# A graph network in one kernel: second dense and first pre stage between the blocks of the second sums, run marks and loads elsewhere

## The chip, the cores and the metric

One core of one Trainium2 chip. The time is the device time of one execution, in microseconds (us), as the median over runs. Engines: TensorE (PE; PEld are its weight loads), VectorE (DVE), ScalarE (ACT), GpSimd (POOL) and SyncE (SP). Each is programmed by hand and they are ordered by semaphores alone.

## The reference

3125 nodes with 128 features, 100000 edges sorted by `dst`, 13 weight blocks. Two SAGE layers, then two PNA layers:

```
mean = segment_sum(x[src], dst) / max(deg, 1)
h    = relu(x @ Ws1 + mean @ Wn1 + b1)                      # sage0
y    = h @ Ws2 + mean(h) @ Wn2 + b2                         # sage1, mean(h) over the same edges
x    = layernorm(x + y)
for l in 0, 1:                                              # PNA, residual on its input
    xi, xj = x @ Wpre[:F], x @ Wpre[F:]                     # pre
    e = xi[dst] + xj[src] + b_pre
    agg = [mean(e), max(e), min(e), std(e)] per dst         # sums and extremes
    out = [x, agg, agg * amp, agg * att] @ Wpost ... @ Wlin # post
    x' = layernorm(out) (relu in layer 0) + input
result = layernorm(x + x')
```

## The kernel before

The nodes are 25 blocks (`NT`) of 125 rows (`NB`), taken in 5 groups (`NG`) of 5 tiles (`GT`). A segment sum is a product with counts: for every pair of blocks a 125 x 125 matrix of edge counts. A block's 25 matrices are an 800 KB tile A, stored in DRAM as `counts`. The rows are split into three bf16 parts (`take_apart`, tile XS), so a block of sums is 25 x 3 = 75 matmuls of 128 columns, `add_block` at L1139.

The order of the stages, with the times of the profile:

- 0 to 401 us: the edges are sampled and the counts are made block by block (`make_block`), and the first sums (those of sage0) run along with them. A block's counts and its `picks`, which select a row for each edge's source in the scans, are stored to DRAM.
- 401.75: the last block of the first sums (L1189 waits for all the block's counts). Beside it VectorE runs `mark_runs` (L1623 to 1650, 398.9 to 410.6): where a node's run of edges begins in the 128 slices of edges; part of it (`whole`) is of use only for inputs that take a branch not taken here (`general_sums`; `flagged` loads the flag).
- 412 to 447: sage0. For each group TensorE turns X and the means (`dense`, L1424), ScalarE copies each turned tile group out (L815), TensorE multiplies it by the weights (L1432), all through one bank pair `turn`. VectorE adds the bias, cuts at zero and splits (`hidden`, L2073 to 2079).
- 447 to 594: the second sums, `sums(1, F)`, a `Fori` over pairs of blocks on TensorE (L1199 to 1209) and ScalarE (L789 to 802), which scales a block's sums and loads the A of the block after the next. Beside it VectorE's `draw_rest` (L1942 to 2036) lists the edges beyond the picks, and POOL gathers 25 + 3 small pieces of these lists (L1106 to 1112). VectorE then waits for the end of the sums.
- 597 to 626: sage1, as sage0, with residual and layer norm on VectorE (`result`, `scaled`, L2086 to 2110; the roots are taken on ScalarE). 627 to 642: `dense_pre` (L1383 to 1409), the pre stage of PNA layer 0 (pre0), whose output Y is stored as the gather table; `rows_ready` counts its groups.
- 643 to 1300: the main scan of layer 0 (`main_scan`). POOL gathers rows of the table four at a time (L1078), VectorE scans them for maximum and minimum (L2170), TensorE selects and lifts rows by the picks (L1267, L1279) and adds the blocks of its sums. It has 91 slots (`NSLOT`); `SPLIT_SLOT` and others say what is done in which. SP loads the picks into a ring of three parts of 640 KB at the slots' start. The scan's last rows go to `rest_history`; a short chain (carries, `fix`) follows, then POOL gathers the rows in which the nodes end, 25 gathers (L1044), 5 to each of 5 semaphores `ext_in`.
- `post(0)` to 1396, pre1 to 1413, then X + H on VectorE (L2178) ahead of the main scan of layer 1 (to 2071), `post(1)` to the end.

## Time and profile before

| | us |
|---|---|
| median of 3 runs (2171.25 to 2175.35) | 2171.25 |
| span of the profiled execution | 2193.7 |
| PE busy | 1471.8 |
| DVE busy | 1424.0 |
| POOL busy | 804.2 |
| ACT busy | 502.9 |

The profiled execution took 22.45 us more than the median, so its times are compared with each other and the median is given beside them. Share of the chain that ended last: DVE 36%, PE 31%, POOL 1%. Times in the rows count from the span's start; "idle before <-releaser" is how long an engine had waited and what ended the wait, "issue" means that the profile shows no cause. A matmul with f32 operands appears twice in a count (x10 for 5 products).

### The profile page before, as it was taken

What the parts mean: (1) busy time and instruction counts of PE and PEld (TensorE: products, weight loads), DVE (VectorE), ACT (ScalarE), POOL (GpSimd) and SP (SyncE); (2) the same over time, 40 slices, a digit from 0 to 9 for tenths busy, and PEclk for the clock granted to TensorE, in tenths of its full rate; (3) what the DMA queues carried; (4) which work ended last, traced back from release to release, by engine and by line L of the source; (5) the groups of instructions that cost most, each with busy time, mean ns of one, the idle gap of its engine ahead of it and who ended that gap; (6) DMA issues with size and microseconds to landing.
All of it is one profiled execution on the core that took longest, in us unless ns stands there. A gap on an engine that the chain in (4) does not pass through costs nothing.

```text
span 2193.7 us, 30278 instructions
## 1 busy us (share of the span) xinstructions
PE 1471.8 (67%) x11250; PEld 1048.3 (48%) x11250; DVE 1424.0 (65%) x2879; ACT 502.9 (23%) x1074; POOL 804.2 (37%) x831
## 2 busy tenths in 40 slices
PE   0277777667854777678677755457777777877553
PEld 0166777657842444445444543324444445544432
DVE  7899999691066665557556645666655566665447
ACT  3367677300031011111111110310111111111101
POOL 4400000032015455455554523155454555546230
PEclk9889898878986898889898887868888888888777
DMA  5223333234433455455555531344554555555320
GB/s 116 89 120 138 146 138 138 83 112 148 135 106 98 156 177 169 145 176 194 181 172 168 177 112 54 98 150 160 176 171 151 192 173 178 196 165 158 109 89 24
DMA packets 126239, 309.36 MB, mean 141 GB/s; under 512 B 21744, under 2 KB 73408, under 8 KB 125742
## 3 DMA queue, kind: packets, MB, share of 16 engines
q1 hardware_dynamic: 75216, 145.00, 18.7%
q10 hardware_dynamic: 23470, 105.20, 13.7%
q0 software_dynamic: 27440, 57.77, 9.8%
q8 instruction: 56, 0.92, 0.2%
q14 instruction: 57, 0.47, 0.1%
HBM read 167.18 MB, written 140.75 MB: 140 GB/s over the span
## 4 chain that ended last, share of the span: by engine, by line
DVE 36%; PE 31%; another core or an unknown queue 16%; issue 8%; DMA 4%; ACT 2%; POOL 1%; ACTq 1%; DVEq 0%; SPq 0%; POOLq 0%
PE ps L1139 14%; PE ps L1267 6%; DVE accs L2141 5%; DVE scanned L2170 4%; DVE accs L2123 4%; DVE scanned L1682 3%; DVE scanned L1679 3%; DVE scanned L1688 3%; PE ps L1279 2%; DMA A<-counts 2%; PE ps L1164 2%; PE ps L1367 2%; PE ps L1432 1%; DVE S L1655 1%
## 5 line engine op out<-in xcount | busy, mean ns | idle before, releaser
L1078 POOL DMA_INDIRECT scanned<-table,rest_idx x688 | 674.0, 980 | 796.7 <-DMA rest_history<-scanned 327.9
L1139 PE MATMUL ps<-big,A 125*128 125x128 bf16 (+1 forms) x7500 | 772.5, 259 | 104.6 <-issue 81.8
L1139 PEld LDWEIGHTS ps<-big,A 125*128 125x128 bf16 x7500 | 623.6, 104 | 249.6 <-issue 139.8
L1267 PE MATMUL ps<-S,big 126*128 126x500 bf16 (+1 forms) x1050 | 282.1, 413 | 264.1 <-DVE accs L2141 184.2
L2141 DVE TENSOR_TENSOR accs<-accs,ps 128x1000 f32<-128x1000 f32 (+1 forms) x154 | 166.8, 1083 | 402.4 <-remote 313.5
L2170 DVE SCALAR_TENSOR_TENSOR scanned<-scanned,rest_neg 128x256 f32<-128x256 f32 x688 | 331.8, 482 | 32.5 <-issue 6.0
L1267 PEld LDWEIGHTS ps<-S,big 126*128 126x128 bf16 x1050 | 102.6, 107 | 387.8 <-DVE accs L2141 205.7
L1164 PE MATMUL ps<-scanned 128*128 128x150 bf16 x1050 | 116.2, 253 | 76.1 <-DVE scanned L1688 75.1
L2123 DVE TENSOR_TENSOR accs<-accs,ps 128x1000 f32<-128x1000 f32 (+1 forms) x154 | 166.0, 1078 | 1.8 <-DVE MS L1796 1.1
L1096 POOL IOTA Y<- 128x784 int32 x1 | 0.8, 786 | 362.8 <-DVEq L1944 362.8
L1164 PEld LDWEIGHTS ps<-scanned 128*128 128x128 bf16 x1050 | 87.6, 132 | 92.5 <-issue 73.2
L752 ACT COPY MS<-ps 128x128 f32<-128x128 f32 x50 | 13.3, 265 | 513.3 <-remote 281.0
L777 ACT ACTIVATE A<-ps,tiny 128x450 bf16<-128x450 f32 x175 | 109.7, 635 | 88.0 <-PE ps L1164 50.2
L1279 PE MATMUL ps<-S,lift 128*128 128x500 bf16 (+1 forms) x350 | 101.9, 370 | 34.8 <-DVE accs L2123 20.1
L1367 PE MATMUL ps<-weights,scanned 128*128 128x384 f32 x200 | 88.8, 574 | 53.2 <-DVE scanned L2223 43.7
L891 ACT ACTIVATE scanned<-scanned 128x512 f32<-128x512 f32 x172 | 104.7, 621 | 65.6 <-DMA scanned<-table,rest_idx 59.3
L1682 DVE TENSOR_TENSOR scanned<-scanned,H 128x900 bf16<-128x900 bf16 x175 | 108.7, 621 | 0.0
L1679 DVE TENSOR_TENSOR scanned<-scanned,H 128x750 bf16<-128x750 f16 x175 | 95.2, 544 | 10.6 <-PE ps L1164 10.3
L864 ACT ACTIVATE operands_t<-operands_t 128x128 f32<-128x128 f32 x50 | 15.5, 309 | 373.0 <-DVE operands_t L1789 200.9
L762 ACT ACTIVATE A<-A,tiny 128x640 bf16<-128x640 bf16 x125 | 99.6, 819 | 0.4 <-DVE S L1655 0.4
L1688 DVE TENSOR_TENSOR scanned<-scanned,H 128x768 bf16<-128x768 bf16 x175 | 96.5, 552 | 0.0
L1367 PEld LDWEIGHTS ps<-weights,scanned 128*128 128x128 f32 x200 | 38.9, 216 | 79.2 <-DVE scanned L2223 52.0
(384 smaller groups left out, 1409.8 us busy)
## 6 DMA issues: line engine op xcount, KB each, us to landing
rest_history<-scanned SPq DMA_DIRECT2D x172, 512.0 KB
A<-counts ACTq DMA_DIRECT2D x75, 800.0 KB
S<-picks SPq DMA_DIRECT2D x60, 640.0 KB
picks<-S ACTq DMA_DIRECT2D x25, 800.0 KB
counts<-A ACTq DMA_DIRECT2D x25, 800.0 KB
scanned<-table,rest_idx POOLq DMA_INDIRECT x688
table<-Y SPq DMA_DIRECT2D x10, 320.0 KB, 2.6
S<-picks SPq DMA_DIRECT2D x10, 160.0 KB
```

Source lines behind the costliest of these rows:

```text
L1078: nc.gpsimd.indirect_dma_start(out=lanes[:, r, s, 0:F], out_offset=None, in_=tables[1 + l], in_offset=bass.IndirectOffsetOnAxis(ap=rest_id ...
L1139: m = nc.tensor.matmul(acc[:, bank, 0:width], A[0:NB, slot, a, :], XS[0:NB, a, c, 0:width], start=a == 0 and c == 0, stop=a == NT - 1 and ...
L1164: m = nc.tensor.matmul(acc[:, h, at:at + CODES], hot_s[:, h, :, t], hot_c[:, h, t], start=t % WT == 0, stop=t % WT == WT - 1)
L1267: m = nc.tensor.matmul(ps[:, bank + h, 0:len(blocks) * NB], XS[0:NB + 1, a, c, 0:F], pick[0:NB + 1, part % RING, 0:len(blocks), a % PART, ...
L1279: m = nc.tensor.matmul(ps[:, bank + h, 0:len(blocks) * NB], lift[:], pick[:, part % RING, 0:len(blocks), a % PART, 0:NB], start=False, sto ...
L1367: m = nc.tensor.matmul(acc[:, b % GT, 0:3 * F], lhs_ext[:, SLOT[b % GT], h * P:(h + 1) * P], weights[:, w + 4 + 3 * h:w + 7 + 3 * h, :] .r ...
L1679: v.tensor_tensor(plain_s[:, h, 0:NB], iota_s[:, 0:NB], by_step(lows, n).unsqueeze(1).to_broadcast([P, NB, PT]), ALU.is_equal)\
L1682: v.tensor_tensor(hot_c[:, h].rearrange("p t (c u) -> p t c u", u=2), iota_c.rearrange("p (c u) -> p c u", u=2).unsqueeze(1) .to_broadcast ...
L1688: v.tensor_tensor(hot_s[:, h], plain_s[:, h], by_step(heavy, n).unsqueeze(1).to_broadcast([P, P, PT]), ALU.mult)\
L2123: v.tensor_tensor(top[:, :, 0:cols], top[:, :, 0:cols], ps[:, bank:bank + 2, 0:cols], ALU.max)\
L2141: v.tensor_tensor(low[:, :, 0:cols], low[:, :, 0:cols], ps[:, bank:bank + 2, 0:cols], ALU.min)\
L2170: v.scalar_tensor_tensor(this, last, rest_neg[:, i:i + 1], this, ALU.add, ALU.max)\
```

## The change

1. `mark_runs` moves from ahead of sage0 into `draw_rest`, and its `whole` part into the flagged branch. The last block of the first sums is split in five, each piece behind its counts (`add_block(0, NT - 1, ..., q * GT, (q + 1) * GT)`).
2. sage0 has two turn banks and four left-hand buffers, both products of a group run together (`turn_item`, `dense_product`), and blocks 0 and 1 of the second sums run piecewise between its groups (`first_pair`).
3. The second sums are written out block by block instead of a `Fori`. From block 16 (`DENSE_FROM`) sage1's turns and products, and pre0 in chunks of 4 tiles, run between the blocks; the last group, two chunks and five tiles of pre0 follow behind. ScalarE's `second_sums` and VectorE's `result`, `add_chunk`, `scaled` follow that order; the end of `draw_rest` becomes `place_rest`, behind them.
4. POOL waits for its 25 small gathers after every fourth.
5. SP loads the first picks as soon as they are stored, and those of layer 1 right behind main scan 0. ScalarE loads the first two A of each layer's sums at the end of the second sums and before `post(0)`.
6. The 25 gathers of `post` count on semaphores in runs of 1, 2, 4, 8, 10 (`END_RUNS`). The first split goes into slot 1 of the scan, X + H into its slot 0.

The diff, cut:

```diff
+XH_SLOT = 0
...
-SPLIT_SLOT = {1: 2, 3: 3, 5: 4}
+SPLIT_SLOT = {0: 1, 1: 2, 3: 3, 5: 4}
...
+DENSE_TURN = {"sage0": [4, 6], "sage1": [4]}
+CHUNK_TILES = 4
+CHUNKS = (NT - GT) // CHUNK_TILES
+DENSE_FROM = NT - 9
...
+END_RUNS = [range(0, 1), range(1, 3), range(3, 7), range(7, 15), range(15, NT)]
+END_RUN_OF = {b: i for i, r in enumerate(END_RUNS) for b in r}
...
+            def first_picks(l):
+                for n in range(RING):
+                    load_part(l, n)
             def main_scan(l):
                 loads = {}
-                for n in range(NPARTS):
-                    loads.setdefault(0 if n < RING else LAST_USE[n - RING] + 2, []).append(n)
+                for n in range(RING, NPARTS):
+                    loads.setdefault(LAST_USE[n - RING] + 2, []).append(n)
...
             general_sums(0)
+            general_sums(1)
+            for w in range(2):
+                sp.wait_ge(a_stored[w], 16 * (1 + 2 * ((NT + 1 - w) // 2)))
+            first_picks(0)
+            sp.wait_ge(runs_marked, 1)
+            sp.dma_start(saved_idx, idx).then_inc(saved, 16)
+            sp.dma_start(saved_neg, neg).then_inc(saved, 16)
...
+                if l == 0:
+                    first_picks(1)
...
+            act.wait_ge(dense_in, 1)
+            load_block(0, 0)
+            load_block(1, 1)
+            for i in range(2 * NG):
+                lhs_copy("sage0", i)
             general_sums(1)
...
+                if l == 0:
+                    load_block(0, 0)
+                    load_block(1, 1)
...
+                if b % BATCH == BATCH - 1:
+                    pool.wait_ge(rest_in, 16 * (b + 1))
...
+            for q in range(NG):
+                pe.wait_ge(counts_made, (NT - 1) * NG + q + 1)
+                add_block(0, NT - 1, 2, 0, F, q * GT, (q + 1) * GT)
...
+                    if l == 0 and s == 0:
+                        pe.wait_ge(rows_ready, NG)
...
+                    run = END_RUNS[END_RUN_OF[b]]
+                    if b == run[0]:
+                        pe.wait_ge(main.ext_in[END_RUN_OF[b]], 16 * len(run) * (l + 1))
...
+            def turn_item(d, source, i):
+                g, banks = i // 2, DENSE_TURN[d]
+                if i >= len(banks):
+                    pe.wait_ge(copied, ITEM_BASE[d] + i - len(banks) + 1)
+                turn_tiles(dense_turn[banks[i % len(banks)]], source, g * GT, (g + 1) * GT).then_inc(turned, 1)
+            def dense_product(d, g, at):
+                pe.wait_ge(copied, ITEM_BASE[d] + 2 * g + 2)
+                pe.wait_ge(evac, EVAC_BASE[d] + g)
+                for t in range(GT):
+                    for q in range(2):
+                        m = nc.tensor.matmul(dense_out[:, t, :], lhs[2 * (g % 2) + q][:, t * P:(t + 1) * P],
+                                             weights[:, at + q, :], start=q == 0, stop=q == 1)
+                        if t == GT - 1:
+                            m.then_inc(product, 1)
+            def first_pair(g):
+                for b in range(2):
+                    if g == 0:
+                        pe.wait_ge(a_in[b], 16)
+                    pe.wait_ge(parts_ready, 2 + g)
+                    add_block(1, b, b, b, F, g * GT, (g + 1) * GT)
...
+            pe.wait_ge(dense_in, 1)
+            pe.wait_ge(sums_out, NT + 2)
+            turn_item("sage0", flat(X[:]), 0)
+            turn_item("sage0", flat(MEAN), 1)
+            for g in range(NG):
+                if g + 1 < NG:
+                    turn_item("sage0", flat(X[:]), 2 * g + 2)
+                    turn_item("sage0", flat(MEAN), 2 * g + 3)
+                dense_product("sage0", g, W_SAGE[0])
+                if g > 0:
+                    first_pair(g - 1)
+            general_sums(1)
+            first_pair(NG - 1)
+            for b in range(2, NT):
+                pe.wait_ge(a_in[b % 2], 16 * (1 + b // 2))
+                add_block(1, b, b % 2, b % 2, F, 0, NT)
+                j, odd = divmod(b - DENSE_FROM, 2)
+                if j < 0:
+                    continue
+                if not odd:
+                    if j > 0:
+                        dense_product("sage1", j - 1, W_SAGE[1])
+                    if j > 1:
+                        turn_chunk(j - 2)
+                    turn_item("sage1", flat(H[:]), 2 * j)
+                else:
+                    if j > 1:
+                        use_chunk(j - 2)
+                    pe.wait_ge(sums_out, NT + 2 + GT * (j + 1))
+                    turn_item("sage1", flat(MEAN), 2 * j + 1)
+            pe.wait_ge(sums_out, 2 * NT + 2)
+            turn_item("sage1", flat(MEAN), 2 * NG - 1)
+            use_chunk(CHUNKS - 3)
...
+            dense_product("sage1", NG - 1, W_SAGE[1])
+            for c in range(CHUNKS - 2, CHUNKS):
+                turn_chunk(c)
+                use_chunk(c)
+            pe.wait_ge(x1_ready, NG)
+            turn_tiles(dense_turn[0], flat(X[:]), NT - GT, NT).then_inc(pre_turned, 1)
+            pe.wait_ge(pre_copied, CHUNKS + 1)
+            pe.wait_ge(rows_ready, CHUNKS - 1)
...
                 dve.sem_inc(found, 1)
+                mark_runs()
+                dve.sem_inc(runs_marked, 1)
...
+                link(v.tensor_scalar(CHUNK, restI, P * REST - 1.0, 1.0, ALU.min, ALU.add))
                 dve.sem_inc(pe_go, 1)
-                dve.wait_ge(small_mm, 5)
-                link(v.tensor_scalar(lanem[:], turn_u[:, P:2 * P], BIG, -BIG, ALU.mult, ALU.add))
+            def place_rest():
+                dve.wait_ge(small_mm, 4)
+                link(v.tensor_scalar(lanem[:], rest_lanes, BIG, -BIG, ALU.mult, ALU.add))
...
             evacuate("sage0", hidden)
-            dve.sem_inc(parts_ready, 1)
+            general_sums(1)
             draw_rest()
...
             for g in range(NG):
-                result(g, mark, need, first=g == 0)
-            scaled(NG - 1, mark, need)
+                result(g, mark, need)
+                if g >= 2:
+                    add_chunk((0, 1, 3)[g - 2])
+                scaled(g, mark, need)
+                if g == NG - 2:
+                    add_chunk(2)
+            add_chunk(CHUNKS - 1)
+            split_rows(0, 0)
+            place_rest()
+            dve.wait_ge(pre_product, CHUNKS + 1)
+            link(v.tensor_tensor(tiles(Y[:], NG - 1), last_out, over_n(V_BPRE[0], GT), ALU.add))
+            dve.sem_inc(rows_ready, 1)
...
+                    if l == 1 and s == XH_SLOT:
+                        link(v.tensor_tensor(X[:], X[:], H[:], ALU.add))
+                        dve.sem_inc(xh_ready, 1)
```

Two places in the order of instructions. First, **TensorE, sage0** (`ident` turns a tile group, `weights` multiplies it, `big,A` is a block of the second sums). Before, the end of sage0 and the loop of the second sums:

```order
L1424 MATMUL ps<-ident,MS 128x128 x5
L1432 MATMUL ps<-weights,scanned 128x128 x5
L1207 UNCONDITIONAL_BRANCH
L1207 ISA
L1136 REGISTER_ALU
L1139 MATMUL ps<-big,A 128x128 x75
L1136 REGISTER_ALU
L1139 MATMUL ps<-big,A 128x128 x75
L1207 REGISTER_ALU
L1207 COMPARE_AND_BRANCH
```

Of the change, two groups of sage0:

```order
L1461 MATMUL ps<-ident,X 128x128 x5
L1461 MATMUL ps<-ident,MS 128x128 x5
L1478 MATMUL ps<-weights,scanned 128x128 x10
L1194 MATMUL ps<-big,A 128x128 x30
L1461 MATMUL ps<-ident,X 128x128 x5
L1461 MATMUL ps<-ident,MS 128x128 x5
L1478 MATMUL ps<-weights,scanned 128x128 x10
L1194 MATMUL ps<-big,A 128x128 x30
```

Each group now turns the next group's two items ahead of its own product, and 30 of the 150 matmuls of blocks 0 and 1 stand behind each product.

Second, **TensorE, end of the second sums.** Before, the last block, the three small matmuls and the first turn of sage1:

```order
L1139 MATMUL ps<-big,A 128x128 x75
L1444 MATMUL ps<-small,scanned 128x25
L1445 MATMUL ps<-small,scanned 128x24
L1446 MATMUL ps<-ident,tiny 128x128
L525 TENSOR_LOAD flagI
```

Of the change, blocks 21 and 22 with what runs around them (C holds the turned tiles of pre0):

```order
L1478 MATMUL ps<-weights,scanned 128x128 x10
L1461 MATMUL ps<-ident,X 128x128 x4
L1461 MATMUL ps<-ident,H 128x128 x5
L1194 MATMUL ps<-big,A 128x128 x75
L1505 MATMUL ps<-weights,C 128x128 x4
L1461 MATMUL ps<-ident,MS 128x128 x5
L1194 MATMUL ps<-big,A 128x128 x75
L1478 MATMUL ps<-weights,scanned 128x128 x10
```

Turns, products and chunks of pre0 stand ahead of blocks that wait for nothing but their A; before, all of them stood behind the last block.

## Rows read from the trace of the kernel before

**Rows 1.** Busy time by stretches; columns us, PE, PEld, DVE, ACT, POOL busy (instructions), PEclk, DMA share, GB/s

```profile
467.80:521.00 53.20, 36.24 (x451) 29.98 (x452) 33.56 (x56) 2.38 (x7) 31.14 (x28) 0.74 0.33 108
521.00:594.00 73.00, 69.44 (x1204) 67.41 (x1204) 0.00 (x0) 5.69 (x16) 0.00 (x0) 1.00 0.51 169
594.00:643.40 49.40, 31.95 (x229) 28.73 (x228) 29.98 (x108) 13.93 (x26) 0.00 (x0) 0.90 0.07 20
643.40:1300.20 656.80, 474.58 (x2820) 301.41 (x2820) 404.54 (x696) 101.92 (x256) 336.34 (x344) 0.86 0.51 166
```

**Rows 2.** Chain of waits, 385 to 455 us; columns start, us, what ran

```profile
401.75 7.10 PE ps L1139 x75
...
413.73 1.96 PE ps L1432 x10
...
417.54 2.50 PE ps L1432 x10
...
440.86 1.40 PE ps L1432 x10
...
447.37 4.76 DMA A<-counts
```

**Rows 3.** Timeline of ScalarE, 396 to 425 us; start, us, ..., [idle before <-releaser]

```profile
401.72 0.35 ACTq L768 DMA_DIRECT2D counts<-A  x1
...
412.99 0.69 ACT L815 COPY scanned<-ps 128x640 f32<-128x640 f32 x1 [3.73 <-PE ps L1424]
```

**Rows 4.** Timeline of TensorE, 385 to 486 us

```profile
439.37 0.71 PE L1424 MATMUL ps<-ident,MS 128*128 128x128 f32 x5
...
463.09 4.36 PE L1139 MATMUL ps<-big,A 125*128 125x128 bf16 x75 [0.85 <-DMA A<-counts]
...
485.41 0.58 PE L1139 MATMUL ps<-big,A 125*128 125x128 bf16 x4 [0.92 <-issue]
```

**Rows 5.** Timeline of POOL, 460 to 520 us

```profile
468.97 0.97 POOL L1107 DMA_INDIRECT icol<-rest_rows,icol  x1 [19.20 <-DMA rest_rows<-Y]
...
507.40 0.94 POOL L1112 DMA_INDIRECT Y<-rest_lists,slices  x1 [0.30 <-issue]
```

**Rows 6.** DMA queues, 467.8 to 521 us; packets, MB, share of 16 engines

```profile
q10 hardware_dynamic: 864, 4.92, 26.7%
q0 software_dynamic: 992, 0.54, 4.9%
```

**Rows 7.** DMA queues, 643.4 to 1300.2 us

```profile
q8 instruction: 22, 0.36, 0.2%
```

**Rows 8.** Chain of waits, 592 to 660 us

```profile
620.93 0.84 DVE Y L2092
...
626.40 0.83 DVE Y L2092
```

**Rows 9.** Timeline of POOL, 640 to 650 and 1412 to 1421 us

```profile
647.11 1.03 POOL L1078 DMA_INDIRECT scanned<-table,rest_idx  x1 [138.77 <-DMA table<-Y]
...
1413.12 1.09 POOL L1078 DMA_INDIRECT scanned<-table,rest_idx  x1 [70.34 <-DMA table<-Y]
...
1417.20 3.33 POOL L1078 DMA_INDIRECT scanned<-table,rest_idx  x1 [0.30 <-issue]
```

**Rows 10.** Chain of waits, whole span

```profile
1300.16 2.59 DMA rest_history<-scanned
...
1420.18 11.75 DMA S<-picks
...
2070.90 2.63 DMA rest_history<-scanned
```

**Rows 11.** Timeline of POOL, 1310 to 1318 us

```profile
1311.80 0.97 POOL L1044 DMA_INDIRECT big<-rest_history,icol  x1 [1.88 <-DMA rest_history<-fix,fixI]
...
1316.83 0.95 POOL L1044 DMA_INDIRECT big<-rest_history,icol  x1 [0.30 <-issue]
```

**Rows 12.** Waits: engine, tile and line, what released them; total us, times, longest us

```profile
DVE accs L2141 <- remote: 313.5, 46, 14.0
```

More of the change, by code:

```diff
@@ L468, in __init__ @@
                 self.fix_out = sem(name + "fix_out")
[L469 removed]
+                self.ext_in = [sem(name + "ext_in")] if looped else [sem(name + f"ext_in{i}") for i in range(len(END_RUNS))]
                 self.start = sem(name + "start")
@@ new lines, in use_chunk @@
+            def use_chunk(c):
+                pe.wait_ge(pre_copied, c + 1)
+                if c == 1:
+                    pe.wait_ge(x1_ready, 3)
+                elif c > 1:
+                    pe.wait_ge(rows_ready, c - 1)
+                for t in range(CHUNK_TILES):
+                    m = nc.tensor.matmul(chunk_out[:, t, :], x_turned[:, c * CHUNK_TILES + t, :],
+                                         weights[:, W_PRE[0] + 1, :], start=True, stop=True)
+                m.then_inc(pre_product, 1)
@@ L1446, in _ @@
-            nc.tensor.matmul(turn_u[:, P:2 * P], lane_whole.to_broadcast([P, P]), ident[:], start=True, stop=True)\
-                .then_inc(small_mm, 1)
-            general_sums(1)
-            dense(1, "sage1", [flat(H[:]), flat(MEAN)], [W_SAGE[1], W_SAGE[1] + 1],
-                  [(0, F, True, False), (0, F, False, True)])
-            for l, inp in ((0, X), (1, H)):
-                dense_pre(l, f"pre{l}", flat(inp[:]), (x1_ready, h_ready)[l])
+            pe.wait_ge(dense_in, 1)
+            pe.wait_ge(sums_out, NT + 2)
@@ new lines, in _ @@
+            dense_product("sage1", NG - 1, W_SAGE[1])
[6 more added lines that the diff above has]
+            pe.wait_ge(rows_ready, CHUNKS - 1)
+            for t in range(GT):
+                m = nc.tensor.matmul(last_out[:, t, :], x_turned[:, NT - GT + t, :], weights[:, W_PRE[0] + 1, :],
+                                     start=True, stop=True)
@@ L1453, in _ @@
+            m.then_inc(pre_product, 1)
+            for l in range(2):
+                if l == 1:
+                    dense_pre(1, "pre1", flat(H[:]), h_ready)
                 main_scan(l)
@@ L1894, in general_sums @@
                     if g > 1:
-                        for i in range(NG):
-                            dve.wait_ge(main.ext_in[i], 16 * GT * (g - 1))
+                        for i, run in enumerate(END_RUNS):
+                            dve.wait_ge(main.ext_in[i], 16 * len(run) * (g - 1))
                         dve.sem_inc(reload_ask, 1)
```

298 lines of the change are left out of this document (147 added, 151 removed).

## The prediction

> **What bounds the kernel now.** I first read the busy times by stretches, to see which stages could give time at all, then the chain of waits, to see what ends each of them, and last the timelines of the engines at the places that the change touches.
>
> The stretches [rows 1] tell three things. From 521 to 594 us, in the second sums, TensorE is busy 69.44 of 73.00 us at a granted clock of 1.00: 1204 matmuls, so 60.6 ns each and 4.55 us for a block's 75. That part is bound by TensorE. From 467.8 to 521 us the same loop does 451 matmuls in 53.20 us. At 60.6 ns they need 27.3, so 25.9 us are lost, at a clock of 0.74. From 594 to 643.4 us no engine is full: TensorE 31.95, VectorE 29.98 and ScalarE 13.93 of 49.40 us, and the DMA share is 0.07. There the engines wait for one another in turn, which is what another order of work can mend. The scan from 643.4 to 1300.2 us has POOL, VectorE and TensorE interleaved; the change leaves its body alone.
>
> What are the 25.9 us? TensorE stands idle or creeps ("<-issue", [rows 4]: 4 matmuls in 0.58 us, where 75 took 4.36 at 463.09), while POOL issues 28 gathers between 468.97 and 508.3 [rows 5]. The block loads moved 4.92 MB in that time and POOL's queue only 0.54 MB [rows 6], so it isn't bandwidth. The stall goes with POOL issuing indirect transfers whose landing nobody awaits.
>
> In the chain [rows 2], the last block of the first sums (75 matmuls, 7.10 us) starts only when all its counts are made; the dense stage follows, then a bare load of 4.76 us, then the second sums. The main scans run from POOL's first gather to the last store: 647.11 to 1300.16 and 1413.12 to 2070.90 [rows 9, 10].
>
> **The sum** is made against the profiled execution, whose span is 2193.7 us. That is 22.45 above the median of 2171.25, and I take that offset over unchanged.
>
> *Stage A, until block 2 of the second sums starts (463.09 before, [rows 4]).* The last block in five pieces: the store of its counts is issued at 401.72 [rows 3], so the last piece is cast by then, and 15 matmuls (7.10 x 15/75 = 1.4) end at 403.1 instead of 408.85. `mark_runs` leaves the path here (it goes into `draw_rest`, beside the second sums). ScalarE then waits for that store (about 4.8, as the load of the same 800 KB, 4.76 [rows 2]), issues two loads and reaches its first copy at about 409 instead of 412.99 [rows 3]. Both turns are ready, so two copies (0.69 each) and both slow products (1.96 + 2.50, the first group's before [rows 2]) end at 414.9 instead of 420.0. From there a group costs TensorE two turns of 0.71 [rows 4], two products of 1.38 to 1.40 [rows 2] and now 30 matmuls of blocks 0 and 1 at 58 ns (4.36/75), together 5.93 us. Before, the last product ended at 442.26, four groups after the first, 5.55 each. VectorE's 5.0 us a group (442.26 to the load's issue at 447.3) fit under 5.93. So the last product ends at 414.9 + 23.7 = 438.6, its group is split at 443.6, and block 2's load follows the last pieces of block 0: 1.1 + 4.8, start at 449.6. **Gain 13.4.** The wait for the first loads of A disappears, since they were issued before the first copy.
>
> *Stage B, blocks 2 to 24.* Before: 463.09 to 593.8 = 130.7 us, of which 23 x 4.55 = 104.6 are work and 26.1 the stall. After: POOL waits for its landings after every fourth gather. No row shows that wait's effect. Bounds: it changes nothing (26 lost), or it removes all of it (0). I take 5 lost, because the same loop loses nothing as soon as POOL is silent [rows 1], and at most four gathers are in flight now. Added on TensorE before the last block: 9 turns (9 x 0.71 = 6.4), 4 products (4 x 2.76 = 11.0), 3 chunk turns of 4 tiles (1.7) and 2 chunk products (2.0): 21.1. They absorb about 1.8 of waits for A. Sum 104.6 + 5 + 21.1 - 1.8 = 128.9. **Gain 1.8**, and the last block ends at 578.5. So the interleaving alone costs here; what it buys comes next. The gathers move with `mark_runs` (11.7 us, 398.9 to 410.6, now ahead of them on VectorE) and have six waits of a landing each; VectorE should be ready at about 533, as TensorE gives the first of sage1's products. From then a group is due every two blocks (9.1 us), and VectorE needs 5.47 (626.40 - 620.93, [rows 8]) and short adds, so it catches up 3 us a group.
>
> *Stage C, from the last block to the last row of the first table.* Before 49.4 us [rows 1]. After: the last MEAN turn, copy, chunk, small matmuls and product 6.5; VectorE's group 5.5 and root 0.5, so the last `x1_ready` 12.5 after the last block. Then VectorE adds chunk 4, splits and places (0.7 + 2.6 + 1.5 = 4.8), which covers TensorE's last turn, copy and product (2.8), and the last add is 0.85: 18.2. **Gain 31.2**, the largest term. Rows are ready at 596.7 instead of 643.2.
>
> *Main scans and post stages.* Picks loaded early don't start layer 0's scan sooner, since its first rows come by POOL's gathers: 0, with bounds -2.6 (the split that moved into slot 0) and +5. The 25 gathers for `post` come 1.26 us apart (1311.80 to 1316.83 for four, [rows 11]), and the first group was due after five. With runs of 1, 2, 4, 8, 10 it is due after one: 4 x 1.26 = 5.0, of which I count 4, for each layer. In layer 0 the early picks of layer 1 (three of 640 KB) and two A loads (800 KB) now collide with that chain of short transfers. The nearest row is the gather at 1417.20, which took 3.33 instead of about 1 us beside such loads [rows 9]; I take 3 off. **Post 0: +1** (bounds -8 to +5), **post 1: +4**.
>
> The Trainium skill ("DMA: Bandwidth & Descriptors", section "Queues, rings and completion order") says that a DMA engine goes round its queues a packet at a time, so a short transfer would wait for a packet, not for a load. By that the toll is under 1 instead of 3, and the saving 2 larger. The row at 1417.20 speaks against it, so I keep 3.
>
> Layer 1's scan waited 11.75 us for picks at 1420.18 [rows 10], and it had 3.5 us of X + H before it. Yet it took only 657.8 us from POOL's first gather to its end, against 653.1 in layer 0: the scan absorbs most of that. **+3**, with bounds 0 and 15.
>
> Sum: 13.4 + 1.8 + 31.2 + 1 + 3 + 4 = 54.4. Profiled 2139.3, median **2117**. That is far over the 0.2% (4.3 us) that a measurement of this kernel can tell from no change.
>
> **The rivals.**
> 1. *The stall beside the gathers stays, or is only in profiled executions.* For: no row shows that the wait on `rest_in` helps, and the offset of 22.45 between profile and median is close to 21. Against: VectorE's waits of the same kind inside the scans total 313.5 us [rows 12], far above 22.45, so such stalls are no artifact of profiling. Either way 21 us of the gain go: 2138. Chance 0.20.
> 2. *Slower: straight-line code stalls TensorE on instruction fetch.* The loop over 23 blocks becomes 23 x 75 x 2 = 3450 instructions. TensorE's fetch queue brought 22 packets for 5640 instructions (2820 matmuls with their weight loads) in the first scan [rows 1, 7], so 256 a packet, and 13.5 packets are added, one per 9.7 us of sums. Its price if all the scan's unexplained waits were fetches: 313.5 over the two scans' 44 packets = 7.1 us each. Then 13.5 x 7.1 = 96 is lost and 54 gained: 2213. It decides above 54/13.5 = 4.0 us a packet. Against: the stretch from 467.8 to 521 stalls in a loop that fetches nothing new. Chance 0.06. The Trainium skill ("Runtime: NRT & Kernel Launch", section "Instruction fetch mechanics") has blocks of 256 instructions too and calls the cost of crossing one mostly hidden; by that this rival's price is about 0.
> 3. *VectorE comes late.* A landing beside two queued block loads can take 9.5 (2 x 4.76) instead of 2.5 us; six of them add 42 to POOL, so VectorE starts sage1's groups at 575, and stage C keeps about four groups of 5.47: 22 less, minus what A's waits give back, 2131 to 2140. Against: the gathers' data is 0.54 MB. Chance 0.09.
> 4. *The order changes but another wait takes it all up*: 2171. Nothing in [rows 1] speaks for it; 0.01.
>
> **How the numbers follow.** The forecast has 0.64. Its own range is 2098 (18.6 more: scan 1 by 12, post 0 by 4, no split cost 2.6) to 2131 (post 0 by 9 and scan 1 by 3 worse, 2 more in C). The range to 2146 takes in rivals 1 and 3, the first with 8 us of such costs besides, and leaves out rival 2 and the tails. Faster 0.64 + 0.20 + 0.09 = 0.93, same 0.01, slower 0.06.
>
> **What would show it.** Right: TensorE without gaps while POOL gathers at about 475 to 525; last block of the second sums ending near 579; POOL's first scan gather near 600 instead of 647.11; no wait for S<-picks at the start of layer 1's scan; `post`'s first turn of EXT one landing behind the first of the 25 gathers, not behind the fifth. Wrong: matmuls in fours with "<-issue" gaps (rival 1 if beside gathers, rival 2 if they come with q8's packets all through the sums), VectorE's first add of sage1 after 570 (rival 3), or a scan whose length from first gather to last store grows over 653.1 and eats the earlier start.

## The result, and the profile after

| | before | changed |
|---|---|---|
| median, us | 2173.3 (4 runs, 2171.25 to 2180.13) | 2110.75 (4 runs, 2081.93 to 2119.21) |
| ratio | | 0.9623, 95% interval 0.9553 to 0.9692 |
| profiled span | 2193.7 | 2117.5 |
| TensorE's fetch packets (q8) | 56 | 69 |

Faster, by 62.5 us between the medians and by 82 by the ratio, which leaves the two runs of the changed kernel with the lowest clock out. The interval of the ratio is 67 to 97 us; 54 were forecast. By the ratio the time is 2091 us, below the range's low end of 2098.

Busy time by stretches, changed kernel (columns as in [rows 1]): blocks 2 to 16 of the second sums, blocks 17 to 24 with the work between them, and the stage behind them.

```profile
446.40:527.60 81.20, 69.19 (x1127) 66.45 (x1128) 52.08 (x91) 5.14 (x14) 29.52 (x28) 0.96 0.53 174
527.60:579.80 52.20, 49.56 (x727) 49.06 (x726) 15.40 (x59) 10.08 (x21) 0.00 (x0) 0.97 0.38 127
579.80:606.30 26.50, 19.62 (x111) 17.06 (x111) 17.23 (x53) 12.47 (x21) 0.00 (x0) 0.76 0.27 82
```

The stage behind the sums fell from 49.4 [rows 1] to 26.5 us. Timeline of TensorE, changed kernel, at the places of stage A and the tail (beside [rows 4]):

```profile
400.47 4.36 PE L1194 MATMUL ps<-big,A 125*128 125x128 bf16 x75 [1.84 <-ACT A L792]
...
411.86 2.69 PE L1478 MATMUL ps<-weights,scanned 128*128 128x128 f32 x20
...
446.47 10.18 PE L1194 MATMUL ps<-big,A 125*128 125x128 bf16 x150 [3.14 <-DMA A<-counts]
...
579.61 2.45 PE L1478 MATMUL ps<-weights,scanned 128*128 128x128 f32 x20
...
586.73 2.05 PE L1505 MATMUL ps<-weights,C 128*128 128x128 f32 x8 [2.07 <-DVEq L2233]
...
589.85 4.08 PE L1478 MATMUL ps<-weights,scanned 128*128 128x128 f32 x20
```

Block 2 starts at 446.47 (forecast 449.6). The rows at 579.61 and 589.85 are the products of sage1's groups 3 and 4: group 3's comes only behind the last block. The row at 586.73 is a chunk of pre0 that waits for VectorE to add the chunk before it. Timeline of POOL, changed kernel (beside [rows 9, 11]): the first gather of either scan, the two transfers of the fix and the first of the 25 gathers.

```profile
609.11 0.94 POOL L1130 DMA_INDIRECT scanned<-table,rest_idx  x1 [92.24 <-DMA table<-Y]
...
1254.93 1.03 POOL L1085 DMA_INDIRECT fix<-rest_history,fixI  x1 [30.20 <-DMA rest_history<-scanned]
1263.16 1.03 POOL L1090 DMA_INDIRECT rest_history<-fix,fixI  x1 [7.21 <-DVEq L1969]
1265.85 0.97 POOL L1096 DMA_INDIRECT big<-rest_history,icol  x1 [1.66 <-DMA rest_history<-fix,fixI]
...
1366.56 1.12 POOL L1130 DMA_INDIRECT scanned<-table,rest_idx  x1 [69.74 <-DMA table<-Y]
```

And the start of layer 1's scan, before and after (timeline of VectorE). I count the first slot from its `take_low`, in which VectorE takes over the slot's minimum (the rows at 1441.51 and 1374.61). It lay 28.4 us behind POOL's first gather (1413.12, [rows 9]) and lies 8.0 behind it now, with X + H following instead of leading.

```profile
1416.23 3.49 DVE L2178 TENSOR_TENSOR X<-X,H 128x3200 f32<-128x3200 f32 x1
1434.84 1.20 DVE L2120 COPY accs<-ps 128x1000 f32<-128x1000 f32 x1 [15.12 <-PE ps L1267]
1441.51 1.20 DVE L2138 COPY accs<-ps 128x1000 f32<-128x1000 f32 x1 [4.57 <-remote]
```

```profile
1374.61 1.19 DVE L2275 COPY accs<-ps 128x1000 f32<-128x1000 f32 x1
1375.72 3.48 DVE L2337 TENSOR_TENSOR X<-X,H 128x3200 f32<-128x3200 f32 x1
```

### The profile page after: what moved, and what is told of

It reads as the page before. It is cut to its first block, busy times and chain, and to the rows that moved or that the text cites. A ratio compares the mean times of both kernels' runs of the same rounds, so it can differ in the third digit from the quotient of the medians.

```text
span 2117.5 us, 30101 instructions
## 1 busy us (share of the span) xinstructions
PE 1474.9 (70%) x11248; PEld 1055.0 (50%) x11248; DVE 1422.7 (67%) x2870; ACT 502.6 (24%) x1075; POOL 807.6 (38%) x831
## 3 DMA queue, kind: packets, MB, share of 16 engines
q1 hardware_dynamic: 75216, 145.00, 19.4%
q10 hardware_dynamic: 23470, 105.20, 14.2%
## 4 chain that ended last, share of the span: by engine, by line
PE 33%; DVE 33%; another core or an unknown queue 16%; issue 11%; DMA 3%; POOL 2%; ACT 2%; ACTq 1%; DVEq 0%; POOLq 0%
PE ps L1194 15%; PE ps L1307 6%; DVE accs L2278 5%; DVE scanned L2307 4%; DVE accs L2260 3%; DVE scanned L1796 3%; DVE scanned L1793 3%; DVE scanned L1802 3%; PE ps L1319 2%; PE ps L1220 2%; PE ps L1410 1%; PE ps L1278 1%; PE ps L1280 1%; DVE S L1769 1%
## 5 line engine op out<-in xcount | busy, mean ns | idle before, releaser
L1410 PE MATMUL ps<-weights,scanned 128*128 128x384 f32 x200 | 91.7, 589 | 54.4 <-DVE scanned L2361 40.9
L782 ACT COPY MS<-ps 128x128 f32<-128x128 f32 x50 | 13.3, 265 | 457.9 <-PE ps L1194 256.4
L1793 DVE TENSOR_TENSOR scanned<-scanned,H 128x750 bf16<-128x750 f16 x175 | 95.1, 544 | 12.3 <-PE ps L1220 12.2
```

Source lines behind the costliest of these rows:

```text
L1410: m = nc.tensor.matmul(acc[:, b % GT, 0:3 * F], lhs_ext[:, SLOT[b % GT], h * P:(h + 1) * P], weights[:, w + 4 + 3 * h:w + 7 + 3 * h, :] .r ...
L1793: v.tensor_tensor(plain_s[:, h, 0:NB], iota_s[:, 0:NB], by_step(lows, n).unsqueeze(1).to_broadcast([P, NB, PT]), ALU.is_equal)\
```

## The experiments

The runs fell on chips of two kinds, and this decides how each is read. On three chips the kernel before took 1782 to 1784 us, and its traces show no wait on a releaser that they can't name. In the other three sets of runs (the result's, r5 to r8, r17 and r18) it took 2139 to 2173, and in either kernel VectorE waited some 240 to 310 us in the scans on a releaser that the trace doesn't show (line of the waits' view, changed kernel, beside [rows 12]):

```profile
DVE accs L2278 <- remote: 240.0, 41, 12.8
```

I call them chips without and with the stall. Medians are only compared within a chip. "Scan body" is from the first slot's `take_low` to the end of the last slot.

### The two kernels again

> The kernel before, for a trace from the same chip as the runs beside it. If the scans' bodies (first slot to last) differ by chip and not by kernel, they take here what the changed kernel's take on this chip, within 10 us; the first slot of layer 1's scan comes 28 us after POOL's first gather on any chip.

> The changed kernel on the same chip. Stage by stage against the kernel before: block 2 of the second sums 17 us earlier, rows ready 37 to 50, the start of layer 1's scan 20 shorter, the bodies of the scans equal within 10 us each. If instead the change shortened the bodies, both are 7 us or more shorter here too.

> The changed kernel once more, to see how far its runs spread. If the extra gain over the forecast (the two main scans together 41 us shorter than before, where 3 were forecast) belongs to the change, the scans are again about 642 and 628 us from POOL's first gather to the last store. If a part is chance of the run, the bodies behind the first slots (about 634 and 620 us) come back nearer to 641 and 629, and the time lies 10 to 20 us higher. The ratio to before should be 0.960 to 0.976.

r9 and r10 ran on one chip without the stall: 1782.24 and 1755.29 us, ratio 0.9845 (0.9817 to 0.9872). r1, on another such chip: 1751.66, 0.9833 (0.9805 to 0.9860), where 0.960 to 0.976 was expected from the result; its scans can't be held against the result's. Stretches of r9, then of r10, each with blocks 2 to 14, blocks 15 to 24, the time behind the sums and the start of layer 1's scan:

```profile
457.90:518.30 60.40, 56.09 (x975) 54.46 (x975) 37.78 (x73) 4.72 (x13) 30.48 (x28) 1.00 0.60 196
518.30:563.20 44.90, 43.10 (x750) 41.88 (x751) 0.00 (x0) 3.36 (x10) 0.00 (x0) 1.00 0.49 165
563.20:619.00 55.80, 34.49 (x235) 30.81 (x232) 33.48 (x112) 17.90 (x31) 0.05 (x1) 0.84 0.13 35
...
1184.10:1209.40 25.30, 6.17 (x18) 2.56 (x18) 8.41 (x9) 6.55 (x11) 19.77 (x19) 0.53 0.74 252
```

```profile
440.80:506.00 65.20, 59.08 (x976) 57.71 (x976) 44.50 (x67) 4.78 (x13) 24.69 (x24) 0.95 0.55 184
506.00:567.70 61.70, 57.93 (x875) 57.42 (x875) 23.00 (x82) 10.46 (x22) 4.46 (x5) 0.97 0.44 143
567.70:596.90 29.20, 22.33 (x128) 18.39 (x125) 18.71 (x55) 14.60 (x24) 0.00 (x0) 0.77 0.28 86
...
1169.90:1177.90 8.00, 5.25 (x18) 2.30 (x18) 2.37 (x4) 5.40 (x9) 6.17 (x7) 0.79 0.16 43
```

The kernel before loses almost nothing beside its 28 gathers here: 975 matmuls in 60.40 us at a clock of 1.00, where the recorded chip lost 25.9 us. So the change costs TensorE 21.6 us from block 2 to block 24 (457.9 to 563.2 against 440.8 to 567.7) and gives 26.4 back behind it (up to POOL's first gather). POOL's first gather came 22 us earlier (619.0 against 596.9); 37 to 50 were expected, and the difference is the 21.6. The scan bodies are 6.7 and 4.8 us longer in the changed kernel (459.6 and 461.1 against 466.3 and 465.9): a split moved into both, X + H into the second. r1's were 462.1 and 468.5. Layer 1's first slot came 25.2 us behind its gather in r9 (28 were expected) and 8.1 in r10.

### POOL's wait on its gathers

```diff
-                if b % BATCH == BATCH - 1:
-                    pool.wait_ge(rest_in, 16 * (b + 1))
```

> The changed kernel without POOL's wait after every fourth of the 25 small gathers. Theory (gathers in flight that nobody awaits stall the second sums): blocks 2 to 16 lose about 26 us again instead of 12.9, so rows are ready 10 to 13 us later. Rival (the wait does nothing, the loss depends on how the loads of A lie against the gathers): 606 within 3 us.

> The changed kernel without that wait, again. On a chip with the stall: theory 90 to 94 us for blocks 2 to 16, where five traces with the wait gave 76 to 85; rival 76 to 85. On a chip without: 75.

> The kernel before with nothing but POOL's wait after every fourth small gather. Theory on a chip that shows the stall (scan bodies over 600 us): blocks 2 to 16 take 13 us less than in the kernel before on this chip, about 81 instead of 94. Rival 1 of the forecast: no change, within 3 us. On a chip without the stall (bodies near 465 us) both say 0.

> The kernel before for a trace beside the next runs. On a chip with the stall (scan bodies over 600 us): blocks 2 to 16 of the second sums take about 94 us as in the recorded profile; on a chip without it about 69.

> The kernel before with POOL's wait after every fourth small gather, again. On a chip with the stall: theory 81 us for blocks 2 to 16 instead of 94; rival 1 of the forecast 94 within 3. On a chip without: 70 and 69, no difference in time.

All five fell on chips without the stall, where both theories say nothing happens, and nothing clear of noise did: r3 1747.44 us (0.9803, 0.9776 to 0.9829), r15 1753.9 (0.9846, 0.9817 to 0.9876), the kernel before with the wait added 0.9996 twice (r12, r14; 0.9979 to 1.0014 and 0.9975 to 1.0017), r13 as before 1783.84. Without the wait the changed kernel was 4.2 us faster on r1's chip (r3; the intervals overlap), so the wait costs little or nothing there. The last two runs, both on a chip with the stall, test it (r17 has three edits, told below; up to block 13 only the wait and the marks' place differ from r18):

> The changed kernel with sage1 from block 14, no wait of POOL on its small gathers, and the marks of the runs ahead of sage0. Theory: VectorE is free near 500 instead of 528 us, the stall of 8.3 us ahead of the second product (dense from 14 alone) goes, the stage behind the last block takes 20 instead of 29 us: rows ready about 8 to 10 us earlier than in the changed kernel, and so the whole time. Rival: something else in that stage takes it up (0 to 2 us). On a chip with the stall, blocks 2 to 14 lose 13 us more without the wait if the wait is what helped; if not, they take what the changed kernel's take within 4 us.

> The changed kernel on the same chip, to set the run before it against. Gather window and tail as in the runs so far: last matmul of the sums to POOL's first gather 29.4 us, first gather 7.9 us ahead of the first slot.

Timeline of TensorE and stretch of blocks 2 to 13 in r17 (no wait), then in r18 (wait):

```profile
466.51 2.07 PE L1194 MATMUL ps<-big,A 125*128 125x128 bf16 x34 [0.82 <-DMA A<-counts]
468.75 0.39 PE L1194 MATMUL ps<-big,A 125*128 125x128 bf16 x4 [0.17 <-issue]
...
489.86 0.73 PE L1194 MATMUL ps<-big,A 125*128 125x128 bf16 x10 [0.92 <-DMA A<-counts]
491.27 0.40 PE L1194 MATMUL ps<-big,A 125*128 125x128 bf16 x4 [0.68 <-issue]
```

```profile
445.70:525.00 79.30, 63.74 (x899) 58.43 (x900) 45.35 (x83) 4.04 (x11) 31.15 (x28) 0.83 0.41 134
```

```profile
473.47 0.49 PE L1194 MATMUL ps<-big,A 125*128 125x128 bf16 x6 [0.28 <-issue]
474.20 1.90 PE L1194 MATMUL ps<-big,A 125*128 125x128 bf16 x31 [0.24 <-issue]
476.79 8.55 PE L1194 MATMUL ps<-big,A 125*128 125x128 bf16 x150 [0.68 <-DMA A<-counts]
```

```profile
446.60:505.90 59.30, 53.64 (x900) 51.78 (x900) 44.47 (x67) 4.04 (x11) 22.09 (x20) 0.97 0.59 190
```

The same 900 matmuls take 79.3 us without the wait and 59.3 with it. Without it they often come in fours, as in [rows 4], while POOL gathers back to back (459.7 to 499), though not all the time: 152 of them run through from 476.74 to 488.9. With it the stall ends when POOL stands (timeline of POOL, r18), and doesn't come back beside the next eight gathers (477 to 492):

```profile
472.71 0.94 POOL L1160 DMA_INDIRECT icol<-rest_rows,icol  x1 [0.30 <-issue]
477.16 1.70 POOL L1160 DMA_INDIRECT icol<-rest_rows,icol  x1 [3.50 <-DMA icol<-rest_rows,icol]
```

Five more traces with the wait on such chips (the result's, r5 to r8) take 65.8 to 73.7 us for blocks 2 to 14; r18 takes 65.9, r17 84.3 and the kernel before 85.5. So with the wait this stretch is 11 to 20 us shorter, and the pair r17 and r18 lies at the upper end. r8 has the marks where r17 has them, but keeps the wait, and takes 73.7: the marks' place isn't what costs r17 its time.

### The work between the blocks

```diff
                 add_block(1, b, b % 2, b % 2, F, 0, NT)
+            for b in range(DENSE_FROM, NT):
                 j, odd = divmod(b - DENSE_FROM, 2)
-                if j < 0:
-                    continue
```

and the same on ScalarE.

> The changed kernel with sage1 and the chunks of pre0 in the same order and with the same banks, but all behind the last block of the second sums. Forecast's theory (the work between the blocks costs 19.5 us there and saves 31 behind them): rows are ready 12 us later, ratio to the changed kernel 1.005. Rival (VectorE's 5.5 us a group is the bound of that stage either way, and what saved time is that pre0 follows in chunks): the sums end about 21 us earlier (near 559), the stage behind them takes about 41 instead of 26.5 us, and rows are ready within 5 us of 606.

1764.2 us, ratio 0.9898 (0.9873 to 0.9923), against 1751.66 for r1 on the same chip. Stretches of r2 (block 2 to 24; behind the sums), then of r1:

```profile
443.70:552.90 109.20, 100.23 (x1726) 98.00 (x1727) 52.05 (x91) 8.09 (x22) 29.56 (x28) 0.98 0.57 191
552.90:615.00 62.10, 43.50 (x252) 37.59 (x249) 34.06 (x113) 21.67 (x37) 0.02 (x1) 0.78 0.14 41
```

```profile
445.70:570.20 124.50, 114.59 (x1849) 112.76 (x1850) 68.05 (x149) 15.23 (x35) 29.98 (x28) 0.98 0.50 168
570.20:599.80 29.60, 22.73 (x129) 18.79 (x126) 18.70 (x55) 14.61 (x24) 0.01 (x1) 0.77 0.28 85
```

With the work between the blocks (r1) the sums take 15.3 us more and the stage behind them 32.5 less. r2 is late by 15.2 at POOL's first gather, by 12.5 in the median. The account expected 12, and it holds. The rival, by which the chunks and banks alone save the time, expected about 41 us behind the last block and falls: it took 62.1.

### Sage1 two blocks earlier

`DENSE_FROM` is 14, so the product of group 3 and one more chunk stand ahead of the last block.

> The changed kernel with sage1 started two blocks earlier, from block 14, so that the product of group 3 and a chunk stand ahead of the last block. Theory (the stage behind the last block waits for VectorE's group 3, which starts only then): rows ready 6 to 10 us earlier, ratio to before 0.978 to 0.981 on a chip without the stall, where the changed kernel had 0.984. Rival (VectorE isn't free before 528 us, so the first product only waits and TensorE stalls between blocks): 0 to 2 us.

1757.6 us, 0.9842 (0.9820 to 0.9864), where 0.978 to 0.981 was expected: no gain over the changed kernel. The stage behind the sums is 20.0 us instead of 29.4, as expected, but ahead of the second product TensorE waits 8.3 us. The row names ScalarE's copy, and that copy stands behind a root that VectorE asks for in group 0, which it begins only at 535.62, when it is free of `draw_rest` (timelines of TensorE, VectorE and ScalarE, r16):

```profile
540.13 3.86 PE L1480 MATMUL ps<-weights,scanned 128*128 128x128 f32 x20 [8.32 <-ACT scanned L830]
...
535.62 0.82 DVE L2217 TENSOR_TENSOR Y<-ps,vectors 128x640 f32<-128x640 f32 x1
...
539.29 0.21 ACT L823 ACTIVATE small<-small 128x5 f32<-128x5 f32 x1 [11.73 <-DVEq L2185]
```

r17 adds the two edits that free VectorE early (marks ahead of sage0, no wait of POOL). That stall goes and the 20.0 us stay, but on its chip blocks 2 to 13 take 20 more, as told above: first gather at 614.0 instead of r18's 605.5, median 2106.79 against 2078.24 (ratios 0.9879, 0.9832 to 0.9926, and 0.9744, 0.9678 to 0.9809). Of these 28.5 us the traces account for the 8.5 up to the first gather; where the others lie isn't shown, for behind it r17's profiled execution is the shorter one. Sage1 from block 14 with the marks ahead and the wait kept wasn't tried.

### Where the marks are made

```diff
+            mark_runs()
             link(v.tensor_copy(ends_up_to, turn_u[:, P:2 * P]))
...
                 dve.sem_inc(found, 1)
-                mark_runs()
```

> The changed kernel with the marks of the runs ahead of sage0 on VectorE again (without their flagged part). Theory: VectorE isn't waited for before sage0's first sum at about 414.5, the marks end near 408, so sage0 starts as early as before; the small gathers start 6 us earlier. Rows ready within 2 us of 606; what left the path was the flagged part and the unsplit last block, not the marks. Rival (the forecast's wording: the marks leave the path): 6 to 8 us slower.

On a chip with the stall: 2084.16 us, 0.9729 (0.9673 to 0.9785). The marks end well before VectorE is wanted (timeline of VectorE, r8). Block 2 starts 47.2 us behind the start of the first sums' last block (397.50 to 444.70), against 46.0 in the changed kernel (400.47 to 446.47), so their place is worth about 1 us and not the rival's 6 to 8:

```profile
403.34 0.29 DVE L1884 COPY run_ends<-ps 128x128 f32<-128x128 f32 x1
411.74 0.82 DVE L2200 TENSOR_TENSOR H<-ps,vectors 128x640 f32<-128x640 f32 x1 [8.10 <-PE ps L1478]
```

### The start of layer 1's scan

> The changed kernel with the first picks of layer 1 loaded only behind the table's stores. Theory (the scan pays in full for what its first slot waits, because everything behind it follows in a fixed order): from POOL's first gather of layer 1 to the first slot 20 to 25 us instead of 8.0, and the time 12 to 17 us longer, less 3 for the collision ahead of post(0), so 9 to 14 longer. Forecast's theory (the scan absorbs most of it): the first slot is late, but the last store comes at most 4 us later.

> The changed kernel with X + H ahead of the main scan of layer 1 again, picks early. Theory of full price: 3.5 us longer. Rival: it lay beside the gathers and costs nothing, because the first slot waits for picks or rows; 0 within 1 us.

> The changed kernel with the first two A of each layer's sums loaded in the scans again instead of at the end of the second sums and ahead of post(0). Theory: they are needed from slot 6 on, so the scans don't change; the fix gather at the end of scan 0 still collides with the picks (it took 6.6 us, 3.7 before the change). 0 within 2 us. Rival: the bodies of the scans gained (about 7 and 9 us) because these 3.2 MB no longer fall on their first slots; then the scans are 5 to 15 us longer together.

These ran on one chip with the stall: 2082.19 us (0.9745, 0.9692 to 0.9798), 2100.99 (0.9818, 0.9764 to 0.9871) and 2089.61 (0.9703, 0.9627 to 0.9778). No changed kernel ran beside them, and their intervals are wider than what they test. But the stage itself reads clean: from POOL's first gather to the first slot 8.7, 12.2 and 10.6 us. No edit alone brings the old 28.4 back; for r5 alone 20 to 25 were expected. The scan bodies of r7 (612 and 613 us) are not longer than those of the other changed kernels, so its rival, by which the A loads' place gave the shorter bodies, isn't borne out. So I put two together: X + H ahead, then its store, then the picks.

> The changed kernel with the start of layer 1's scan in the old order: X + H first, its store, then the first picks. Theory (either part alone cost 0 to 4 us, since the other left room; together they are the old 28.4 us): first slot 20 us later than in the changed kernel, and the whole time 15 to 20 us longer, since the body doesn't absorb it. Rival (the forecast: the body absorbs most): first slot late, time 3 us longer.

1759.46 us, 0.9866 (0.9841 to 0.9891), on r10's chip (1755.29). The first slot comes 19.4 us behind the first gather instead of 8.1, held by the picks behind the store (chain of waits, r11; `before` has 11.80 there on this chip):

```profile
1172.59 8.56 DMA S<-picks
```

So the stage lost 11.3 us and not the 20 expected; what is left up to r9's 25.2 I put down to the A loads, the one edit not undone here; no run shows it. The median is 4.2 us longer, the span 6.9 (1758.6 against 1751.7). By stages that is 11.3 at this start, -3.2 in post(0), whose short transfers no longer meet the picks, -1.1 in the body, -1.6 in post(1), and 1.5 ahead of them all. The body returns 1.1 of 11.3 us, no more than changed kernels differ by on such chips (r11 464.8, the others 465.5 to 469.9). The medians alone could not have told this: their intervals are about as wide as the difference.

### Runs of the gathers ahead of post

`END_RUNS` is five ranges of five again.

> The changed kernel with the 25 gathers ahead of each post stage counted in runs of five again. Theory of the forecast: the first turn of post follows the first of its gathers by 7.8 us instead of 2.8, and the kernel is 4 to 5 us slower per layer, 8 to 10 in all. Rival (post is bound later by TensorE or VectorE, or the clock, and an earlier start is waited away): the first turn is 5 us later but the post stages end at the same distance from the scans' ends, within 1 us each (115.5 and 123.0 us).

1754.33 us, 0.9835 (0.9810 to 0.9861), r1 1751.66: 8 to 10 us were expected, and there is no difference that this measurement tells. `post(0)` and pre1 together take 96.9 us from the scan's end instead of 97.4; `post(1)` takes 1.7 more. Timelines of TensorE, r1 (first gather at 1084.33), then r4 (1088.22):

```profile
1087.15 0.69 PE L1397 MATMUL ps<-ident,big 128*128 128x128 f32 x2 [14.17 <-DMA big<-rest_history,icol]
...
1104.69 0.44 PE L1397 MATMUL ps<-ident,big 128*128 128x128 f32 x2 [3.61 <-DMA big<-rest_history,icol]
```

```profile
1096.06 1.11 PE L1397 MATMUL ps<-ident,big 128*128 128x128 f32 x4 [18.65 <-DMA big<-rest_history,icol]
```

The first turn comes 2.8 us behind the first gather instead of 7.8, but the fourth run (8 gathers) is due only at 20.4 us and TensorE waits 3.6 for it. With fives, block 8 is reached at about the same distance.

## Why the prediction was right or wrong

| step, us gained | forecast | result's chip | r10 against r9 |
|---|---|---|---|
| A, to block 2 | 13.4 | 16.6 | 17.1 |
| B, blocks 2 to 24 | 1.8 | -2.6 | -21.6 |
| C, to the first gather | 31.2 | 24.0 | 26.4 |
| start and body of scan 0 | 0 | 4.0 + 7.2 | 3.9 - 6.7 |
| post(0), pre1 | 1 | -2.6 | -5.0 |
| start of scan 1 | 3 | 20.4 | 17.1 |
| body of scan 1 | 0 | 9.5 | -4.8 |
| post(1) | 4 | -0.2 | 0.3 |
| sum | 54.4 | 76.3 | 26.9 |

(Each cell is the difference of the stage's length in the two traces.) The errors have both signs. The median of 2110.75 lies 6 us from the forecast 2117, and that is no confirmation: on the same steps the other kind of chip gives 27 us instead of 54.

**The step that failed is "the scan absorbs most of that. +3".** It was read from two lengths that were nearly equal, 657.8 and 653.1 us. They hid two differences: layer 1's first slot came 16.5 us later (28.4 against 11.9), and its body was 11.8 shorter (630.0 against 641.8). I took the second for an answer to the first. It isn't one. After the change the body of layer 1 is still 14.1 shorter (620.5, 634.6), with no late start to absorb. In r9 the late start is there (25.2 against 11.8) and layer 1's body is 1.5 longer than layer 0's. And r11 shows that of 11.3 us of delay 1 comes back. The start was worth 17 to 20 us: on the result's chip 17.4 more than forecast, of the 21.9 by which the profiles' sum exceeds the forecast. The clue stood in the profile: X + H, its store and the picks in a row, 11.75 us of S<-picks in the chain [rows 10]. r5 to r7 show that any one edit alone leaves little of it, so a sum by parts would have missed it as well.

**The start of scan 0** (forecast 0) gave 4.0 on both kinds of chip. The forecast said that early picks can't start this scan sooner, since its first rows come by POOL's gathers. But the gathers themselves came sooner: ScalarE had the first gathered rows 10.3 us behind POOL's first gather (647.11) while picks and A were being loaded, and has them 6.2 behind it (609.11) now. With the A loads back in the scan and the picks early (r7) the first slot is 0.7 later than in the changed kernel, so most of it is the picks. Timeline of ScalarE, before, then changed:

```profile
657.41 0.63 ACT L891 ACTIVATE scanned<-scanned 128x512 f32<-128x512 f32 x1 [6.48 <-DMA scanned<-table,rest_idx]
```

```profile
615.33 0.63 ACT L943 ACTIVATE scanned<-scanned 128x512 f32<-128x512 f32 x1 [6.87 <-DMA scanned<-table,rest_idx]
```

**The scans' bodies** (forecast 0) gave 16.7 on the result's chip and cost 11.5 on r10's. Most of the cost is the work moved in (a split of 2.6 us into each, X + H, 3.48, into the second): over all traces on such chips layer 0's body takes 460 us in the kernel before and 461 to 466 in changed ones, layer 1's 461 to 465 and 465 to 470. The gain isn't shown to be the change's: seven traces of changed kernels on chips with the stall have bodies of 598 to 635 us, and there is one trace before, 641.8 and 630.0. A spread as wide as the difference leaves it open. Without the bodies the result's profile gives 59.6, near the 62.5 of the medians and the 55 of r18 (0.9744 of 2141.73); that they agree may be chance.

**Stage B was 4 short (it lost 2.6 where 1.8 were to be gained), its mechanism was right, and rival 1 was wrong on the result's chip.** Where nothing stalls, the stretch from block 2 to 24 is 21.6 longer in the changed kernel (forecast 21.1 - 1.8 = 19.3). The work between the blocks is 15.3 of it (r1 against r2). Another 4.8 lie in blocks 2 to 14, where nothing was added: their first 150 matmuls take 10.18 us in r10, where the next 150 take 8.55 (in r9 that slow start, 10.37, fell on blocks 0 and 1, ahead of the stretch), and TensorE is idle for 6.1 us in them instead of 4.3. The difference of 19.0 between the two columns is the stall relieved (forecast 21). Rival 1's other half, that the stall is only in profiled executions, falls too: except for the recorded kernel before, each profile belongs to one of the timed runs, and on chips with the stall that run is the longest of the result's four but the shortest of r17's ten. But on chips without the stall rival 1's gain of 34 is what comes out (27 to 33). I had 0.20 on it as a matter of mechanism, while it is a matter of the chip.

**Stage C was 5 to 7 short** up to the first gather, and 8.3 up to the table's last row, where the forecast ended (26.5 instead of 18.2). The term "turn, copy, chunk, small matmuls and product 6.5" was mis-sized: it measured 14.2 (579.78 to 593.97). I had left out three things. Group 3's product (2.45) stands behind the last block. The chunk after it waits until VectorE has added the chunk before, which it does in the middle of group 3. And beyond that wait TensorE ran mostly at the lower of its two clocks (1.2 GHz): group 4's product took 4.08 us and not 2.45. Stretches of the changed kernel, up to the wait's end and behind it:

```profile
579.80:586.00 6.20, 3.98 (x34) 3.53 (x33) 3.50 (x14) 2.50 (x5) 0.00 (x0) 1.00 0.38 132
586.00:590.00 4.00, 3.27 (x15) 3.31 (x16) 2.77 (x8) 2.09 (x3) 0.00 (x0) 0.57 0.09 26
590.00:594.00 4.00, 4.00 (x24) 4.00 (x23) 0.03 (x1) 0.00 (x0) 0.00 (x0) 0.58 0.51 149
```

r16 has neither the product nor the chunk there; its last product runs at a granted clock of 1.00 in 2.50 us, and the stage takes 20.0.

**Stage A** was 3 to 4 better: ScalarE and the first products lay as forecast (408.93 and 414.55, against 409 and 414.9), but the last product ended at 434.0 and not at 438.6. From the first product's end it took 19.5 us, not 4 x 5.93 = 23.7: the durations that I had added overlap in part (a group took 5.0 to 5.2), and ahead of the last product stand no turns. Its wording that the marks leave the path is mostly wrong: r8 shows that their place is worth about 1 us. What left the path is the flagged part with its matmuls, and the wait ahead of the last block. Unsplit, the block came behind 4.72 us of idleness and took 7.10, at a granted clock of 0.50 in its first 4 us; split, it came behind 1.84 and took 4.36, at 1.00.

**Post** was wrong in its 4 us for each layer: I priced the first wait and not the fourth (r4). The 3 us for the collision came out: from the fix's gather to its store 8.2 us instead of 5.3 (1254.93 to 1263.16, and 1303.58 to 1308.89 before), and r11 gives 3.2 back. (r9's 93.8 us for `post(0)` and pre1 are at the low end of the kernel before, 94 to 96 on such chips, so the table's -5.0 is partly spread.) But the 3 us came out by luck, for the row that they were read from shows something else. The gather at 1417.20 was issued while VectorE ran X + H, the picks' loads only at 1420.18, and A's (1417.26) behind its start. In all 20 traces the one gather issued inside X + H is the only one that takes over 2.5 us (3.28 to 4.09), and it ends 0.8 us behind X + H. It is so in r6 too, with the first picks and A loaded long before (timelines of VectorE and POOL, r6):

```profile
1353.45 3.49 DVE L2315 TENSOR_TENSOR X<-X,H 128x3200 f32<-128x3200 f32 x1
1354.43 3.34 POOL L1130 DMA_INDIRECT scanned<-table,rest_idx  x1 [0.30 <-issue]
```

The rule weighed against it (the Trainium skill, "DMA: Bandwidth & Descriptors", section "Queues, rings and completion order") would have had the short transfers wait for a packet each, by the forecast's estimate under 1 us; this one lost 2.9 us beside 2.5 MB of loads.

**Rival 2** (fetch): the instruction queue q8 brought 13 packets more, as counted (69 against 56), and its blocks still take 4.35 us in straight-line code beside 4.36 in the loop, so the price is about 0. That agrees with the Trainium skill ("Runtime: NRT & Kernel Launch", section "Instruction fetch mechanics"). **Rival 3** didn't occur: VectorE was free at 527.6 (forecast 533), ahead of the first product at 537.3. r16 shows how near it was.

## What to carry to other kernels

Two stages of nearly equal length can hide a late start and a short body: measure the start and the body apart before saying that one absorbs the other. A finer semaphore is worth only what its last coarse run lets through. A long duration beside a load isn't yet a collision with it: look at what every other engine did in the same microseconds. Work moved between bound blocks pays by what it takes off the serial stage behind them (15 us spent, 32 saved), and in r16 how early it could begin was set by the engine that was free last.

## What the runs showed of the hardware that was not expected

The same two kernels run 22% apart on different chips (1784 and 2173 us), and the gain is 1.6 to 1.7% on the one kind and 2.6 to 3.8% on the other. The difference lies in stalls in which TensorE issues its matmuls in fours, 0.7 to 1.4 us apart, while POOL issues indirect transfers, at times with the DMA engines almost idle (0 to 2 GB/s from 491 to 497 us in r17); the scan bodies take 460 to 470 us without them and 598 to 642 with them. Waiting for every fourth gather took 11 to 20 us of it away, and no cost of it could be told where there is no stall. What stalls TensorE there, and why only on some chips, no run here tells.

A gather that POOL issues while VectorE adds X and H (128 x 3200, f32) takes 3.28 to 4.09 us instead of 0.94, in all 20 traces, on either kind of chip.
